# Recurrent kernel: VectorE writes h of the second half of the features in full ahead of its 16-bit high half

## The reference

```python
def _L0_cond_ref(x, h0, Wx, Wh, b):
    xW = jnp.einsum('ntd,dg->ntg', x, Wx) + b
    def step(carry, xw_t):
        prev_h, prev_c = carry
        a = xw_t + prev_h @ Wh
        i = sigmoid(a[:, :H]); f = sigmoid(a[:, H:2*H]); o = sigmoid(a[:, 2*H:3*H])
        g = tanh(a[:, 3*H:])
        next_c = f * prev_c + i * g
        next_h = o * jnp.tanh(next_c)
        return (next_h, next_c), next_h
    ...
return x + _L0_cond_ref(x, cond_1024, Wx, Wh, b)
```

## Time and profile before

| | us |
|---|---|
| median of 3 runs (1845.93 to 1848.51) | 1846.87 |
| the profiled execution's own time | 1846.18 |
| its span | 1844.4 |
| busy: PE / DVE / ACT / POOL | 1689.8 / 1724.7 / 1013.6 / 174.8 |

### The profile page before, as it was taken

How to read it: one execution, slowest core, us unless ns; L and a number is a source line. 1 busy time by engine, 2 the same in 40 slices (tenths; PEclk the granted TensorE clock), 3 DMA queues, 4 the chain that set the end, 5 groups by cost and what they waited for, 6 DMA issues and landing times.

```text
span 1844.4 us, 105808 instructions
## 1 busy us (share of the span) xinstructions
PE 1689.8 (92%) x45212; PEld 1087.2 (59%) x45212; DVE 1724.7 (94%) x10378; ACT 1013.6 (55%) x3992; POOL 174.8 (9%) x539
## 2 busy tenths in 40 slices
PE   6999999999999999999999999999999999999997
PEld 4565555565555556555555655555665555565555
DVE  8999999999999999999999999999999999999998
ACT  5555555555555555555555555555555555555554
POOL 1000000000000000000000000000000000000000
PEclk9999999999999999999999999999999999999999
DMA  5000000000000000000000000000000000000000
GB/s 212 20 21 21 25 23 21 21 26 21 21 25 22 21 21 26 21 21 26 21 21 21 27 21 21 26 21 21 21 26 21 21 24 23 21 21 26 18 12 15
DMA packets 39065, 49.02 MB, mean 27 GB/s; under 512 B 4416, under 2 KB 36160, under 8 KB 38592
## 3 DMA queue, kind: packets, MB, share of 16 engines
q1 hardware_dynamic: 37152, 37.77, 6.6%
q10 hardware_dynamic: 1440, 4.49, 0.6%
HBM read 25.46 MB, written 16.78 MB: 23 GB/s over the span
## 4 chain that ended last, share of the span: by engine, by line
DVE 67%; PE 22%; ACT 8%; issue 3%; DMA 1%; ACTq 0%; DVEq 0%
DVE turned L600 22%; PE acc L386 13%; DVE mailbox L604 13%; DVE products L613 11%; PE acc L392 8%; ACT gates L305 7%; DVE h_halves L628 4%; DVE h_halves L639 4%; DVE gates L622 2%; DVE x_tops L681 2%; DVE h_feat L633 2%; DVE mailbox L618 2%; DVE out_ring L668 2%; DVE x_halves L584 1%; DMA wx<-in_wx 1%
## 5 line engine op out<-in xcount | busy, mean ns | idle before, releaser
L386 PE MATMUL acc<-wh_low,h_halves 128*32 128x256 f16 x16384 | 719.7, 274 | 135.3 <-DVE h_halves L628 130.8
L392 PE MATMUL acc<-wh_high,h_halves 128*32 128x256 f16 x16384 | 719.7, 274 | 0.0
L386 PEld LDWEIGHTS acc<-wh_low,h_halves 128*32 128x32 f16 x16384 | 391.9, 97 | 394.1 <-DVE h_halves L628 380.4
L378 PE MATMUL x_accs<-wx_high,x_halves 128*32 128x512 f16 x8192 | 620.9, 380 | 1.5 <-ACT x_accs L244 1.5
L305 ACT ACTIVATE gates<-mailbox 128x96 f32<-128x96 f32 x1024 | 256.1, 250 | 640.7 <-DVE mailbox L604 637.6
L600 DVE STREAM_TRANSPOSE turned<-acc 128x256 f32<-128x256 f32 x1024 | 458.1, 447 | 30.4 <-PE acc L392 17.8
L392 PEld LDWEIGHTS acc<-wh_high,h_halves 128*32 128x32 f16 x16384 | 350.7, 95 | 105.5 <-issue 0.2
L378 PE MATMUL x_accs<-wx_low,x_halves 128*32 128x512 f16 x4096 | 398.8, 379 | 0.0
L248 ACT ACTIVATE acc<-x_accs,masks 128x512 f32<-128x512 f32 x511 | 334.1, 654 | 0.0
L215 POOL TENSOR_TENSOR o_preact<-turned 128x32 f32<-128x32 f32 x512 | 165.6, 324 | 1650.5 <-DVE turned L600 1650.5
L613 DVE SCALAR_TENSOR_TENSOR products<-gates 128x64 f32<-128x64 f32 x1024 | 231.3, 226 | 61.4
(11 more groups left out here) (92 smaller groups left out, 569.2 us busy)
## 6 DMA issues: line engine op xcount, KB each, us to landing
out<-out_ring SPq DMA_DIRECT2D x128, 128.0 KB, 2.1
x_ring<-in_x SPq DMA_DIRECT2D x120, 128.0 KB, 3.0
wx<-in_wx ACTq DMA_DIRECT2D x4, 512.0 KB, 8.1
wx<-in_wx SPq DMA_DIRECT2D x4, 512.0 KB, 8.0
wh<-in_wh SPq DMA_DIRECT2D x4, 512.0 KB, 16.8
wh<-in_wh ACTq DMA_DIRECT2D x4, 512.0 KB, 17.1
x_ring<-in_x SPq DMA_DIRECT2D x2, 512.0 KB, 16.6
b_rows<-in_b ACTq DMA_DIRECT2D x1, 256.0 KB, 21.3
```

Source lines behind the costliest of these rows:

```text
L378: last = pe.matmul(x_acc[pair % 2][32 * j:32 * j + 32], x_halves[:, pair % (CHUNK // 2), c, half], w[:, c].rearrange("p (n q) g -> p q n g ...
L386: pe.matmul(acc[par][32 * j:32 * j + 32, n, 0:GL], h_halves[1 - par][:, c, 0:2], w_low["wh"][:, c, n * Q + j], start=False, stop=False, sk ...
L392: last = pe.matmul(acc[par][32 * j:32 * j + 32, n, 0:GL], h_halves[1 - par][:, c, 1:3], w_high["wh"][:, c, n * Q + j], start=False, stop=c ...
```

## The change

```diff
@@ -636,6 +636,8 @@
                 def low_of_h(first, blocks, kept):
                     cs = slice(first, first + blocks)
                     dve.wait_ge(h_feat_ready, NG * t + kept)
+                    if kept == 2:
+                        dve.wait_ge(h_high_ready, NG * (t + 1) + kept)
                     dve.tensor_tensor(h_halves[par][:, cs, 2, :], h_feat[par][:, cs, :], h_halves[par][:, cs, 1, :], ALU.subtract)\
                         .then_inc(h_ready, 1)
 
@@ -654,8 +656,9 @@
                 full_h(0)
                 keep_cell(0)
                 low_of_h(0, 2, 1)
+                dve.wait_ge(h_parts_ready[1], 2 * (t + 1))
+                full_h(1)
                 high_of_h(1)
-                full_h(1)
                 keep_cell(1)
                 low_of_h(2, 1, 2)
                 low_of_h(3, 1, 2)
```

## The result

| | before | changed |
|---|---|---|
| median us (runs) | 1846.92 (4) | 1881.63 (4; 1881.02 to 1882.80) |
| the profiled execution's own time | 1846.18 | 1882.80 |
| its span | 1844.4 | 1881.0 |

The ratio is 1.0184, with a 95% interval of 1.0172 to 1.0196. The prediction said 1877.5, in a range of 1862 to 1890.

The account below looks back on a forecast made before the run. It took a loop of dependences through VectorE, TensorE and ScalarE, 3.51 us a step, as the bound. 511 steps x 0.06 = 31 us on the profiled 1846.2 gave 1877, or 1877.5 for the median, range 1862 to 1890.

Parts of the forecast that it names:

- The wait: VectorE, group 1's first subtraction: two waits, the second ending last, taken as 0.10 us, starting it 0.07 later.
- TensorE's surplus of 0.06: TensorE's L426 loads near the end: start 0.12 us after the high half, where a single wait takes 0.06.
- only a bound: VectorE's L604, two waits, starts 0.10 us after the transposition; upper limit only, since L613 holds the engine too.
- rival 1: VectorE's subtractions: the second wait is free, so 1846 to 1850 us, not slower; chance 0.12.
- rival 2: VectorE's subtractions: the second wait costs half, 0.02 to 0.05 us over a single one, 1856 to 1871; chance 0.08.
- The late high half: Group 1's high half ends 0.10 us later; covered by TensorE's matmuls of blocks 0 and 1, cost 0 to 0.01.
- Rival 3: TensorE: high half's cover fails, low parts 0.10 us later, 1897 us; chance 0.08 together with rival 4.
- TensorE's slack: Block 2's loads come 0.07 us later with 0.01 to spare, so matmuls and the next round come 0.06 later.
- The second subtraction: VectorE, block 3: its two waits are long fulfilled while it queues 0.09 us behind the first; costed at nothing.
- rival 4: Both subtractions pay, block 3's loads end late: about 0.09 us a step, 1892; chance 0.08 together with rival 3.
- some 30 us of TensorE waiting for the subtraction: Sign expected in the changed kernel's waits: a new line of TensorE waiting for L639, some 30 us.

Follow-up runs that it names:

- experiment 2: The changed kernel with its swap, but group 1's subtractions wait for the high half first, full h second: 1850.83 us, ratio 1.0030.
- experiment 3: The kernel before, no swap; group 1's subtractions wait for the high half first and full h second, which ends last: 1881.26 us, ratio 1.0198.
- experiment 4: The changed kernel with the second wait on the subtraction of block 2 alone: 1879.82 us, ratio 1.0187.
- experiment 1: The kernel before, order unchanged, with only the second wait added to group 1's two subtractions: 1849.33 us, ratio 1.0024.
- Experiment 5: The changed kernel's swap, but group 1's subtractions have one wait alone, for the high half: 1848.15 us, ratio 0.9999.

## Why the prediction was right

**The wait.** The step that carried the forecast was the second wait that ends last: 0.10 from the end of the writer to the start of the subtraction, 0.07 more than before. The rows after show 0.10, and in the records' medians the subtraction starts 72 ns later against the transposition. The size came from TensorE's surplus of 0.06 in the earlier trace rows, put on VectorE's 0.04. The 0.10 of the earlier trace rows, which the prediction called only a bound because of L613, gave no support: in an ordinary step of the kernel before the same line has one wait and starts just as late.

```profile
1001.11 0.45 DVE L600 STREAM_TRANSPOSE turned<-acc 128x256 f32<-128x256 f32 x1
1001.51 0.23 DVE L613 SCALAR_TENSOR_TENSOR products<-gates 128x64 f32<-128x64 f32 x1
1001.66 0.26 DVE L604 TENSOR_TENSOR mailbox<-turned 128x96 f32<-128x96 f32 x1
```

The transposition ends at 1001.56 and L604 starts 0.10 later. In the records both medians are 104 ns, over 481 steps with one wait and 31 with two, and L604 starts 143 ns behind L613 in both, so the row can't tell one wait from two. The one row that carried the forecast was thus of another engine, and that VectorE pays nearly the same surplus (69 ns) was in part luck. The sentence in VectorE: DVE Perf Modes, The DRAIN you can't avoid, of the Trainium skill, by which a semaphore costs nothing extra, would have given rival 1; it does not carry over to two waits ahead of one instruction, as experiments 2 and 3 show (1850.83 us with the late wait first, 1881.26 with it second). Rival 1 is out for the changed kernel, and so is rival 2.

**The late high half** cost nothing, as costed. Rival 3 fell with experiment 2.

**TensorE's slack.** Of 72 ns 11 were absorbed in all, and 61 ns a step arrived; the prediction had 0.07, with 0.01 to spare. 511 x 0.061 = 31.2 us. The parts are not quite those of the prediction: by the medians, counted from TensorE's first matmul of the step, the loads of block 2 start 67 ns later and their matmuls 46 ns, so 21 ns were to spare, and the transposition comes 55 ns later. Where the 9 ns behind the matmuls and the last 6 come from stays open.

**The second subtraction** was costed at nothing. Its wait moved it by 13 ns (experiment 4), and this stayed hidden; rival 4 did not occur.

**What was missing.** The spans differ by 36.6 us, so 5.4 us more than the sum. It is in 20 long steps of the changed kernel, which are 0.08 to 0.37 us over the median each and 5.5 us together, leaving out the first three steps and 476. No step of the prediction named them; they widened the true cost from 31 to 36 us, still inside the range. They come with second waits, whichever ends last: experiments 1 and 2 have them at an ordinary step of 3505 and 3507 ns, and that is the 4 and 5 us by which they stand over the kernel before. Experiment 5, without second waits, has no more of them than the kernel before.

**The waits in the profile.** I had expected some 30 us of TensorE waiting for the subtraction. The view gives 83.7 us on the weight loads and 2.1 on the matmuls (in the page). The idle time of the loads, 0.16 a step, counts from the end of the load before, which ended early; the cost in time is the 0.05 by which the matmuls slip, which has become 0.06 at the next transposition of group 0.

## What to carry to other kernels

Where an instruction needs two waits, write first the one that is fulfilled last, or drop the other if the later result implies it: here that alone was worth 29 us of 35, and a single wait the rest. A swap of two equal instructions was free; the wait that came with it was not. On a loop that is one chain of dependences, count semaphore instructions as instructions, also those that have no row in the profile.

## What the runs showed of the hardware

**The order of two waits.** In the trace's records the wait written first is carried by the instruction itself, and the one written second by a semaphore instruction in front of it. That instruction starts 38 to 39 ns behind the end of the writer, and VectorE's next instruction 65 to 66 ns behind that, 104 ns in all; with a wait that the instruction carries itself it is 35. If the semaphore instruction is fulfilled early, the ordinary step shows nothing of it (3505 to 3507 against 3506 ns, experiments 1 and 2).

**Every 128th instruction.** Counting all of VectorE's records from 0, semaphore instructions too, the late instruction of a long step is number 63 in its 128, in every one of the 20 steps of the changed kernel. In the kernel before, number 63 falls on the two subtractions of group 1 or the output row 13 times and is never over 6 ns late. In the changed kernel it fell 15 times between the first of these subtractions and the output row, the semaphore instructions between them included, and was 295 to 370 ns late each time; 4 times it fell just behind the output row, 198 to 215 ns late. Ahead of the first of these subtractions it cost nothing anywhere in a step, on that subtraction's own semaphore instruction neither, with one exception (step 486, 0.22 late). The kernel before isn't free of it: just behind the output row number 63 is 0.16 late in steps 200 and 288.

The page's instruction transfers fit a block of 128: 1024 more instructions brought 128 packets instead of 120, one for 128 instructions, and the 512 more of experiment 4 brought 124. No view prints these packets one by one, but the trace's records hold their starts, without the engine. In the 13 cases of the kernel before, packets of this queue start 0.4 to 2.3 us ahead of number 63, and none within 1.5 us behind it; at each of the 20 late instructions one starts 0.66 to 0.96 us behind it. That fits a list that is read less far ahead past a semaphore instruction, which is how I read it. It doesn't fit a late instruction that waits for this packet, since it has started by then; what holds it for 0.2 to 0.37 us stays open. The Trainium skill, in Runtime: NRT & Kernel Launch, Instruction fetch mechanics, describes a refill in blocks of 256 instructions, mostly hidden; here the places repeat at 128, and hidden holds for the kernel before, but for the two steps named, and not beside second waits.

Before, the profile's row for these packets was:

```profile
q14 instruction: 120, 0.98, 0.2%
```
